# Delta rule inputs pipelined over three groups, token-major sums of squares, and fp4 rounding by adding a power of two

## What is computed

```python
p20_read = _p20_scan(hidden, p20_decay_log, p20_theta)
normed_p20 = _rmsnorm(p20_read, vnorm_scale)
q_in = _causal_dwconv_silu(q_in, qconv_w)
queries = (q_in + ramp * p20_q).reshape(b, s, H, HD)
reads = _gated_delta_rule(queries, keys, values, g, beta)
normed_reads = _rmsnorm(reads, mnorm_scale).reshape(b, s, d)
projected = fused @ out_W + out_b
```

```python
xn = xb / scale
idx = jnp.searchsorted(_MID, jnp.abs(xn))
q = _GRID[idx] * jnp.sign(xn) * scale
```

## Time and profile before

| what | value |
| --- | --- |
| median of 3 runs | 4765.77 us (4759.86 to 4777.94) |
| profiled execution | 4746.57 us, its span 4744.7 us |
| TensorE granted clock, mean | 0.883 |
| busy in the span | PE 79%, DVE 59%, ACT 40%, POOL 16% |

### The profile page before, as it was taken

One profiled execution on the slowest core, in us unless ns is written; L12 is line 12 of the kernel. 1 busy time (PEld: TensorE's weight loads), 2 busy tenths in 40 slices (PEclk: granted clock), 3 DMA queues, 4 the chain that ended last, 5 costly groups with the idle time before them and its releaser, 6 DMA issues. The chain is left out here.

```text
span 4744.7 us, 71737 instructions
## 1 busy us (share of the span) xinstructions
PE 3758.3 (79%) x27543; PEld 2577.3 (54%) x27543; DVE 2783.0 (59%) x6776; ACT 1913.5 (40%) x2979; POOL 778.8 (16%) x1058
## 2 busy tenths in 40 slices
PE   5998998998989989969999644577745465997996
PEld 3666666666666667647777311255423332443664
DVE  5756747747747657552222477888679865112673
ACT  2554554545645545533333333322212112332443
POOL 2222222222222122130000000000000032002221
PEclk8999999999999999989999766599857666998997
DMA  5414424424325234200000000000000000001440
GB/s 135 114 38 110 113 52 98 100 51 116 80 64 118 63 83 114 63 35 6 1 1 1 14 0 0 0 1 1 1 5 0 4 0 25 0 0 47 99 98 24
DMA packets 156736, 222.56 MB, mean 47 GB/s; under 512 B 16158, under 2 KB 136350, under 8 KB 139422
## 3 DMA queue, kind: packets, MB, share of 16 engines
q10 hardware_dynamic: 19656, 107.37, 10.3%
q1 hardware_dynamic: 136750, 110.69, 8.6%
HBM read 154.42 MB, written 60.82 MB: 45 GB/s over the span
## 5 line engine op out<-in xcount | busy, mean ns | idle before, releaser
L748 DVE TENSOR_REDUCE enc_mx<-psum 128x2 f32<-128x512 f32 (+1 forms) x1152 | 749.8, 685 | 296.0 <-PE psum L457 292.6
L889 ACT ACTIVATE enc_e<-psum 128x1024 f32<-128x1024 f32 (+1 forms) x768 | 580.9, 808 | 423.5 <-PE psum L476 367.6
L457 PE MATMUL psum<-enc_ks,enc_qs 80*128 80x128 bf16 (+1 forms) x3072 | 459.4, 255 | 124.9 <-DVE enc_mx L748 108.9
L476 PE MATMUL psum<-enc_qs,enc_ks 83*128 83x256 bf16 (+1 forms) x3072 | 383.9, 250 | 20.4 <-DMA enc_qs<-enc_turned_max 15.5
L457 PEld LDWEIGHTS psum<-enc_ks,enc_qs 80*128 80x128 bf16 x3072 | 220.3, 100 | 264.8 <-DVE enc_mx L748 174.7
L487 PE MATMUL psum<-enc_e,enc_v 128*32 128x256 f32 (+1 forms) x6144 | 336.7, 338 | 0.0
L476 PEld LDWEIGHTS psum<-enc_qs,enc_ks 83*128 83x128 bf16 x3072 | 261.9, 99 | 58.2 <-DMA enc_qs<-enc_turned_max 20.1
L1764 ACT ACTIVATE moe_act_h<-psum 128x512 f32<-128x512 f32 x288 | 169.3, 598 | 306.0 <-PE psum L1638 305.8
L1660 PEld LDWEIGHTS psum<-par_s,moe_act_h 128*128 128x128 f32 x2304 | 269.7, 192 | 30.1 <-issue 28.5
L1727 DVE SCALAR_TENSOR_TENSOR moe_acc<-psum,moe_gates,moe_acc 128x128 f32<-128x128 f32 x256 | 72.1, 344 | 345.3 <-PE psum L1660 345.3
L1660 PE MATMUL psum<-par_s,moe_act_h 128*128 128x128 f32 x2304 | 272.6, 275 | 0.0
(11 more groups left out here) (457 smaller groups left out, 7380.3 us busy)
## 6 DMA issues: line engine op xcount, KB each, us to landing
enc_qs<-q_pieces ACTq DMA_DIRECT2D x234, 192.0 KB
enc_ks<-k_pieces ACTq DMA_DIRECT2D x234, 192.0 KB
k_pieces<-enc_pieces SPq DMA_DIRECT2D x240, 128.0 KB, 2.0
q_pieces<-enc_pieces SPq DMA_DIRECT2D x144, 128.0 KB, 2.0
enc_qs<-q_pieces SPq DMA_DIRECT2D x54, 192.0 KB
enc_ks<-k_pieces SPq DMA_DIRECT2D x54, 192.0 KB
rope_qs<-q_pieces ACTq DMA_DIRECT2D x39, 192.0 KB
rope_ks<-k_pieces ACTq DMA_DIRECT2D x39, 192.0 KB
```

The costliest lines, as they stand in the source:

```text
L457: last = T_.matmul(p1[f % 2][:, i * kw:(i + 1) * kw], qs[0:KEYED, slot, h, j * P:(j + 1) * P], ks[0:KEYED, slot, h, 0:kw], start=True, sto ...
L476: last = T_.matmul(p2[ch][:, g], ks[0:SCORED, slot, 4 * T + g, ch * P:(ch + 1) * P], qs[0:SCORED, slot, 4 * T + g, 0:n], start=True, stop= ...
L748: V.tensor_reduce(mx[:, u % 2, j * HEADS + h0:j * HEADS + h0 + n], p1[f % 2].rearrange("p (h k) -> p h k", h=n), AX_X, ALU.max)\
L889: A.activation(e_of(T, ch), p2[ch], ACT.Exp, scale=HD ** -0.5).then_inc(s_e, 1)
```

## The change

Inputs stage: the loop is written out over slots k = -1 to 8. In a slot the group k+1 ("ahead") is rotated, scanned and normed, group k ("now") is convolved and gets its reads, group k-1 ("behind") has its queries and keys normed; `padded` and `conv` have two buffers. The sums of squares are now token-major: the squares are the stationary operand and `heads` (one column per head, 16 wide) or one column of `ones` the moving one, so that root and reciprocal work on 128x128 (queries and keys together) or, for the RMS norm, a POOL power on 128x4. POOL then widens an inverse from one value per head to 8 features (`wide`, 128x512, two a slot), and PE turns it back feature-major by products with the identity. Rotation sums are made by accumulating two products in PSUM. All 16 gate products and sigmoids come first and write straight into `dec_all` and `ka_all`; the first tap of each convolution moves to ACT. The copies of H, `pn`, `dec` and `k` and the clearing of `bv_all` are gone; `padded`'s clearing is twice as wide. The stage now ends with a barrier and a clearing of its semaphores.

Output stage: the same token-major sums; root and reciprocal on 128x64, `invert(k+2)` stands after the normed reads of group k on DVE, POOL widens one inverse a group after adding H, and PE turns it. Sums of group k+2 and the turned inverse of k+1 share the bank that group k's normed reads have just read, so they wait for those.

fp4: x itself is scaled by the inverse (less one unit in 2^24), `powers` cuts out its exponent bits and makes 1.5 times 2^22 times max(power, 1), `cut` adds and subtracts that, which rounds, and `finish` scales. Comparisons, the halved scale and the sign step are gone. Between `begin` and `powers` stand two `meet`, between `powers` and `cut` two more, then `cut`, the norm's statistics, its application, `finish`. New waits before each `begin` are for earlier steps of DVE's own queue.

```diff
+        self.step(dve, V.reciprocal(inv, scale))
+        self.step(dve, V.tensor_scalar(inv, inv, self.LESS, None, ALU.mult))
+        self.step(dve, V.tensor_tensor(self.xn[:, 0:B], x, inv.unsqueeze(2).broadcast_to([P, B, BLK]), ALU.mult))
+
+    def powers(self, dve, B):
+        V, xn, big = self.nc.vector, self.xn[:, 0:B], self.big[:, 0:B]
+        self.step(dve, V.tensor_scalar(big.bitcast(U32), xn.bitcast(U32), 0x7F800000, None, ALU.bitwise_and))
+        self.step(dve, V.tensor_scalar(big, big, 1.0, 1.5 * 2.0 ** 22, ALU.max, ALU.mult))
+
+    def cut(self, dve, B):
+        V, xn, big = self.nc.vector, self.xn[:, 0:B], self.big[:, 0:B]
+        self.step(dve, V.tensor_tensor(xn, xn, big, ALU.add))
+        self.step(dve, V.tensor_tensor(xn, xn, big, ALU.subtract))
+
+    def finish(self, dve, B, out, done):
+        self.nc.vector.tensor_tensor(out, self.xn[:, 0:B], self.scale[:, 0:B].unsqueeze(2).broadcast_to([P, B, BLK]), ALU.mult).then_inc(done, 1)
...
+                if b >= 0:
+                    pool.wait_ge(s_inv, b + 1)
+                    for i in range(2):
+                        if b:
+                            pool.wait_ge(s_qback, 2 * b - 1 + i)
+                        nc.gpsimd.tensor_copy(wide[:, i].rearrange("p (n d) -> p n d", d=HD), inv[:, i].unsqueeze(2).broadcast_to([P, TILES * HEADS, HD]))\
+                            .then_inc(s_wide, 1)
+                if a < GROUPS:
+                    pool.wait_ge(s_var, a + 1)
+                    nc.gpsimd.tensor_tensor(rstd[:], var[:], c.minus_half[:], ALU.pow).then_inc(s_rstd, 1)
...
+            for g in range(GROUPS):
+                for i, name in enumerate(("dec", "beta")):
+                    if g:
+                        pe.wait_ge(s_gate, 2 * g + i - 1)
+                    T_.matmul(bank[6 + i], W[name], c.H[:, grp(g)], start=True, stop=True).then_inc(s_gp, 1)
...
+                    pe.wait_ge(s_qsq, 2 * (b + 1))
+                    pe.wait_ge(s_var, min(a, GROUPS))
+                    for i in range(2):
+                        for t in range(TILES):
+                            at = (TILES * i + t) * HEADS
+                            last = T_.matmul(bank[6][:, at:at + HEADS], qk_sq[:, i, t * P:(t + 1) * P], heads, start=True, stop=True)
...
+                    T_.matmul(bank[0], W["partner"], xs[:], start=True, stop=False)
+                    T_.matmul(bank[0], c.ident, xc[:], start=False, stop=True).then_inc(s_x, 1)
...
+                    for t in range(TILES):
+                        last = T_.matmul(bank[6][:, t:t + 1], ysq[:, t * P:(t + 1) * P], c.ones[:, 0:1], start=True, stop=True)
+                    last.then_inc(s_ysum, 1)
+                    pe.wait_ge(s_rstd, a + 1)
+                    if b >= 1:
+                        pe.wait_ge(s_qk, 2 * b)
+                    for t in range(TILES):
+                        last = T_.matmul(bank[7][:, t * P:(t + 1) * P], rstd[:, t:t + 1].broadcast_to([P, P]), c.ident, start=True, stop=True)
+                    last.then_inc(s_yback, 1)
...
+                    pe.wait_ge(s_wide, 2 * b + 1)
+                    if ahead:
+                        pe.wait_ge(s_yinv, a + 1)
+                    else:
+                        pe.wait_ge(s_qk, 2 * b)
+                    for t in range(TILES):
+                        last = T_.matmul(bank[7][:, t * P:(t + 1) * P], wide[:, 0, t * P:(t + 1) * P], c.ident, start=True, stop=True)
...
+            def convolve(g, j):
+                n = 3 * g + j
+                dve.wait_ge(s_tap, n + 1)
+                out = seqs(conv[:, g % 2, j])
+                for tap in range(1, 4):
+                    V.scalar_tensor_tensor(out=out, in0=padded[:, g % 2, j, :, tap:tap + S], scalar=W["conv"][:, 4 * j + tap:4 * j + tap + 1], in1=out,
+                                           op0=ALU.mult, op1=ALU.add).then_inc(s_conv, 1)
+                    if tap < 3:
+                        dve.wait_ge(s_conv, 3 * n + tap)
+
+            def add_reads(g, j):
+                n = 3 * g + j
+                dve.wait_ge(s_silu, n + 1)
+                dve.wait_ge(s_read, n + 1)
+                out = (flat(mine(q_all, g)), flat(mine(k_all, g)), conv[:, g % 2, 2])[j]
+                V.scalar_tensor_tensor(out=out, in0=bank[(1, 4, 5)[j]], scalar=ramp[:], in1=conv[:, g % 2, j], op0=ALU.mult, op1=ALU.add).then_inc(s_ramp, 1)
+
+            for k in SLOTS_K:
+                now, ahead, behind = 0 <= k < GROUPS, 0 <= k + 1 < GROUPS, 0 <= k - 1 < GROUPS
+                a, b = k + 1, k - 1
+                if ahead:
+                    if a:
+                        dve.wait_ge(s_x, a)
+                    V.tensor_tensor(seqs(xs[:]), seqs(c.H[:, grp(a)]), both(sin), ALU.mult)
+                    V.tensor_tensor(seqs(xc[:]), seqs(c.H[:, grp(a)]), both(cos), ALU.mult).then_inc(s_xin, 1)
+                if now:
+                    convolve(k, 0)
+                if ahead:
+                    dve.wait_ge(s_x, a + 1)
+                    if a:
+                        dve.wait_ge(s_zin, a)
+                    V.tensor_tensor_scan(z[:, 0:S], rad[:], bank[0][:, 0:S], 0.0, ALU.mult, ALU.add)
+                    V.tensor_tensor_scan(z[:, S:GROUP], rad[:], bank[0][:, S:GROUP], 0.0, ALU.mult, ALU.add).then_inc(s_z, 1)
+                    dve.wait_ge(s_z, a + 1)
+                    if a:
+                        dve.wait_ge(s_y, a)
+                    V.tensor_tensor(seqs(zs[:]), seqs(z[:]), both(nsin), ALU.mult)
+                    V.tensor_tensor(seqs(zc[:]), seqs(z[:]), both(cos), ALU.mult).then_inc(s_zin, 1)
+                if behind:
+                    dve.wait_ge(s_root, b + 1)
+                    if b:
+                        dve.wait_ge(s_wide, 2 * b)
+                    V.reciprocal(inv[:].rearrange("p a n -> p (a n)"), root[:].rearrange("p a n -> p (a n)")).then_inc(s_inv, 1)
+                if now:
+                    convolve(k, 1)
+                if ahead:
+                    dve.wait_ge(s_ysum, a + 1)
+                    if a:
+                        dve.wait_ge(s_rstd, a)
+                    V.tensor_scalar(var[:], bank[6][:, 0:TILES], 1.0 / D, 1e-6, ALU.mult, ALU.add).then_inc(s_var, 1)
+                if now:
+                    convolve(k, 2)
+                if ahead:
+                    dve.wait_ge(s_yinv, a + 1)
+                    V.tensor_tensor(pn_all[:, grp(a)], bank[0], yinv[:], ALU.mult).then_inc(s_pn, 1)
+                if now:
+                    for j in range(3):
+                        add_reads(k, j)
+                if behind:
+                    dve.wait_ge(s_qback, 2 * b + 1)
+                    V.scalar_tensor_tensor(out=flat(mine(q_all, b)), in0=flat(mine(q_all, b)), scalar=HD ** -0.5, in1=bank[7],
+                                           op0=ALU.mult, op1=ALU.mult).then_inc(s_qk, 1)
+                if now:
+                    dve.wait_ge(s_ramp, 3 * (k + 1))
+                    dve.wait_ge(s_gate, 2 * (k + 1))
+                    V.tensor_tensor(flat(mine(bv_all, k)), conv[:, k % 2, 2], flat(mine(ka_all, k)), ALU.mult).then_inc(s_bv, 1)
+                    dve.wait_ge(s_bv, k + 1)
+                    V.tensor_tensor(flat(mine(ka_all, k)), flat(mine(ka_all, k)), flat(mine(dec_all, k)), ALU.mult).then_inc(s_db, 1)
+                if behind:
+                    dve.wait_ge(s_qback, 2 * b + 2)
+                    V.tensor_tensor(flat(mine(k_all, b)), flat(mine(k_all, b)), bank[7], ALU.mult).then_inc(s_qk, 1)
+                    dve.wait_ge(s_qk, 2 * b + 2)
+                    dve.wait_ge(s_db, b + 1)
+                    V.tensor_tensor(flat(mine(ka_all, b)), flat(mine(ka_all, b)), flat(mine(k_all, b)), ALU.mult).then_inc(s_ka, 1)
...
-                    pe.wait_ge(s_root, g - 1)
-                T_.matmul(bank[g % 2], W["bones"], sq[:, g % 2], start=True, stop=True).then_inc(s_sum, 1)
+                    pe.wait_ge(s_nr, g - 1)
+                for t in range(TILES):
+                    last = T_.matmul(bank[g % 2][:, t * HEADS:(t + 1) * HEADS], sq[:, g % 2, t * P:(t + 1) * P], heads, start=True, stop=True)
+                last.then_inc(s_sum, 1)
+
+            def turn_inverse(g):
+                pe.wait_ge(s_wide, g + 1)
+                for t in range(TILES):
+                    last = T_.matmul(bank[g % 2][:, t * P:(t + 1) * P], wide[:, g % 2, t * P:(t + 1) * P], c.ident, start=True, stop=True)
+                last.then_inc(s_back, 1)
...
+                    pe.wait_ge(s_nr, k + 1)
                     if k + AHEAD < GROUPS:
                         add_squares(k + AHEAD)
-                    pe.wait_ge(s_nr, k + 1)
+                    if k + 1 < GROUPS:
+                        turn_inverse(k + 1)
```

388 lines of the change are left out of this document (193 added, 195 removed).

## The result

The changed kernel takes 4595.12 us (median of 4 runs, 4586.78 to 4602.12) against 4770.71 for the kernel before (4 runs): a ratio of 0.9644, 95% interval 0.9621 to 0.9667. It is faster by 3.6%. The predicted 4559 us was 36 us too low, the range (4508 to 4614) holds the time. In the profiled executions 4746.57 us became 4586.78: -160 us, where the prediction's sum said -207; by the medians it is -176.

What follows compares the result with a forecast made beforehand. DVE was taken to bound fp4, dependent chains the inputs stage, a ring the output stage. Inputs -135, output -7 and fp4 -65 sum to -207 us: profiled 4746.6 to 4540, median 4765.8 to 4559, range 4508 to 4614.

Steps and rivals of the forecast that it cites:

- the line: Reciprocal cost interpolated between 0.35 us for 32 elements and 3.35 for 512: 0.95 for 128x128, about 0.55 for 64.
- rival (d): POOL's widening copies run far slower than 0.82 us, making the kernel slower: 4804 us at 11 us each; chance 0.02.
- I take 22: Inputs stage: a steady slot takes 22 us, from 19.3 of DVE work plus waits of 1.4 to 6.7; seven make 154.
- ACT's pads, first taps and two table loads a slot, costed at nothing: Inputs stage: 11 us of ACT work in a 22 us slot, priced at zero unless ACT nears the slot.
- my three chains: Inputs slot: rotated z to variance, variance to `pn`, x products to scan; together waits of 1.4 to 6.7 us.
- (a): PE stays at the low clock in the three stages: inputs 258 us, output +1, fp4 -38, time 4636; chance 0.07.
- (b): Inputs stage: the three groups do not overlap, slots of 33 us in place of 22, time 4636; chance 0.05.
- it is a ring: Output stage: reads, PE, `y`, norm and reciprocal form one 10.24 us cycle; shortening the reciprocal gives 9.4, stage -7.
- The bound +3: Output stage: upper bound of its predicted change of -7 us, whose bounds were -14 to +3.
- up to 3.6: fp4: DVE would wait up to 3.6 us a slot for the first two sigmoid-linear outputs.
- Rival (c): fp4 follows a ring on PE and ACT near 29 us, not DVE: +32 us, time 4591; chance 0.08.
- The rule: Inputs stage: exclusion would put 24 widenings on DVE, some 20 us, time 4579; the forecast kept a loss of 5.

Runs made afterwards that it cites:

- sq_first: Changed kernel with ACT's square of the rotated sum ahead of the first silu and its table load in the inputs stage; that stage takes 226.3 us, against 239.6.
- k_turn: Changed kernel with PE's turned inverse for k behind the first, not the third, product of the reads in the inputs stage; that stage takes 232.1 us, against 239.6.
- short_recip: Kernel before, with its output stage inverting only 64 of 512 columns of the root; cycle 10.05 us for 10.24, stage 92.0 us.
- fp4_filled: Changed kernel with fp4's statistics ahead of the first `meet`, plus five unread 512-column products a slot before the norm's transposes; fp4 stage 232.3 us, period 23.9.

## Why the prediction was right, and where it was wrong

**Right.** The sign, the bound and the mechanisms of two stages. DVE was what the inputs and fp4 stages paid for. The pieces of the inputs sum: group 0's rotation on PE after 24.5 us (23 predicted), its chain 12.5 (13), slot 7 14.2 (15), the last slot and barrier 11.2 (11.5). The reciprocal of 128x128 takes 0.95 as taken from the line, that of 64 columns 0.55; POOL's widenings take 0.61 to 1.07 us, and rival (d) is out. Granted clock 0.78 in the inputs stage, above 0.75. fp4's period averages 24.7 (24.5), in part by luck: steady ones are 24.3 to 27.1 and the first and last shorter. DVE's own work there is 20.3 (20.5), the wait before the norm 1.19 (1.3). The rest of the program moved by 6.3 us, under the 10.

**Wrong: the size of a slot** ("I take 22"). From `pn` of group 0 to slot 7 there are 177.3 us, 25.3 a slot: 3.3 too little, seven times, 23 us. DVE's own work was 17.8 to 18, not 19.3 (in a row of steps one starts about 0.6 us after another of 0.69, so the gaps that I added were overlaps); the waits were 6.3 to 9.5, not 1.4 to 6.7. The term that failed is the chain from the rotated z to the variance, 3.9 us at the high clock by my sum, 7.3 in the slot above and 5.9 in the shorter ones, and the entry that hid it is "ACT's pads, first taps and two table loads a slot, costed at nothing". ACT was busy only 104 of 240 us, so by its load it cost nothing; by its order it did, since the square stood behind a table load and a silu. `sq_first` gives 14.5 us of waits back. The second is the k turn behind three products of the reads, which my three chains did not hold at all (`k_turn`, 11.8 us of waits). The third is from the variance to `pn`: 4.4 us, over the 3.1 to 4.0 of the sum, and DVE waited 2.2, since the power took 1.44 and the turn ran at the low clock. Rivals (a) and (b) do not fit this stage: the clock rose from 0.62 to 0.78, and the groups overlapped (b had slots of 33). In the other two stages the clock stayed where (a) has it: 0.68 in the output stage (0.64 before) and 0.69 in fp4 (0.68 before).

**Wrong: the output stage**, in sign. The step that failed is "it is a ring": the reciprocal was on one ring of 10.24 us while a second, through the square and the sums, was as long (`short_recip`). Taking 2.8 us from the first gave 0.2 in a cycle with squares (what the stage gained, it gained at its two ends), and the turned inverse put 2.06 us on the part of PE's queue that both share. The bound +3 had turn and sums at the low clock already; it was too small because it took the whole 3.35 off, and had no wait for ACT's square (1.25 in the cycle above). It also had no term for the stretch ahead of the first `y`, where the sums among the gate products, the gate products at a lower clock (7.27 us for twelve records, 5.69 before) and the turn cost 6.1 us together: the whole +5.7 of the stage. (Of its lower bound, -14, eight cycles of 8.8 give only -12.)

**Nearly right: fp4**, 4.7 us short: first `meet` waits of 1.35 to 4.19 stand where I had "up to 3.6", and the second waits 0.6 more (by the sum's own figures, 14.5 less 9.7, DVE is 4.8 ahead of the second output). They depend on the clock at the down products, which stayed low. Rival (c), a period near 29, is out.

**Compensation.** The three misses (23.3, 12.7, 4.7) all went one way, and with the rest's 6.3 they make up the 47 us between 207 and 160. That the rest moved by 6.3 the same way is chance as far as is known: its code is the same. By the medians the gain is 31 us short.

**The rule weighed.** The Trainium skill ("SBUF — State Buffer", Who interferes with whom) says that a DVE instruction with two SBUF inputs contends with a GpSimd instruction that reads SBUF, and calls the ports that they share an exclusive lock. It says "for the whole instruction" of another mode of DVE; taken for these steps too, two widenings would cost DVE all of their time. Above they take 1.99 us beside taps of 2.68, with 2.32 for the same taps without them. DVE lost 0.36 us and POOL 0.77 (1.99 for twice 0.61), and both were done in 2.7 us, where one after the other they would take 3.5. So the trace does not agree that they exclude each other throughout. Something is shared, but most of the price fell on POOL, and DVE waited for a widened inverse only in the last slot, where the widening ran alone.

## What to carry to other kernels

When a chain is shortened, look for every ring that passes the same two points, and for what is second; if a wait only grows by what was saved, there is a twin. A queue that is half empty can still be late: read where a step stands in its engine's order, against when its input was ready. And after such a change the order of the same instructions may be worth more than the change: here the output stage went from 102 to 108 us with a third less work on DVE, and to 72 by order alone. And price the stretch before a pipeline is full by itself: there the whole loss of that stage stood.

## What the hardware showed that was not expected

PE's clock fell among short gaps. In fp4 a solid stretch of work ahead held it up only into the transposes (the first six records of the down products still took 1.49 us in `fp4_filled`), while three products more, in gaps of 0.7 to 1.35 us, brought all down products to 0.83 and a slot's granted clock from 0.86 to 1.00. Why one slot of three was fast without them stays open. In the output stage order alone raised it from 0.68 to 0.87. Eight added products a slot made the fp4 stage 17 us shorter.

A power on POOL took 1.44 us beside DVE's taps and 1.01 alone: the longer of the two was on the chain to `pn` in every slot but the first, and the sum had 1.0 for it.
